# Seven of 64 scan inputs made by token: ScalarE scales dt * u by B, TensorE turns it back by channel

## What is computed

```python
xz = x @ W_in; x_in, z = split(xz)
u  = silu(conv4(x_in) + conv_b)                 # depthwise, 4 taps
Bm, Cm = split(u @ W_x)                         # 16 + 16 values a token
dt = softplus(u @ W_dt + b_dt)                  # 256 values a token
h  = exp(dt[:, :, None] * A) * h + (dt * u)[:, :, None] * B[:, None, :]   # for each token
y  = einsum('bdn,bn->bd', h, C)
y  = (y + u * D) * silu(z)
x  = layernorm(x + y @ W_out)
x  = layernorm(x + moe(x))                      # 8 experts, top 2, with a capacity
```

## Time and profile before

| | |
|---|---|
| runs | 399.35, 399.61, 401.03 us |
| profiled execution | 401.77 us, its span 400.0 us |
| busy, share of the span | TensorE 72%, VectorE 74%, ScalarE 48%, GpSimd 66% |
| granted TensorE clock, mean | 0.85 of full |
| start of unit 0's first scan | 24.7 us |
| end of the last scan | 269.3 us |
| experts on TensorE | 299 to 374 us |

### The profile page before, as it was taken

How to read it: one execution, slowest core, us unless ns; L and a number is a source line. 1 busy time by engine, 2 the same in 40 slices (tenths; PEclk the granted TensorE clock), 3 DMA queues, 4 the chain that set the end, 5 groups by cost and what they waited for, 6 DMA issues and landing times. The chain is left out here.

```text
span 400.0 us, 4740 instructions
## 1 busy us (share of the span) xinstructions
PE 286.7 (72%) x1420; PEld 200.4 (50%) x1420; DVE 296.2 (74%) x439; ACT 190.8 (48%) x372; POOL 265.0 (66%) x226
## 2 busy tenths in 40 slices
PE   8976888487785848595563897666089999999300
PEld 6435445364563434484351462223088888888300
DVE  2698899989999999889999999995212333333186
ACT  2846576575645694654544345571303333333105
POOL 4517488967788799988979885796520555555512
PEclk9998699979789868968555799899589999999955
DMA  7061069472344354122112311001152443224573
GB/s 209 22 211 52 2 234 277 120 220 86 84 146 122 104 145 156 66 67 95 63 61 69 122 66 54 0 13 42 34 149 68 124 125 116 86 77 131 145 216 105
DMA packets 35784, 42.87 MB, mean 107 GB/s; under 512 B 3862, under 2 KB 26331, under 8 KB 35760
## 3 DMA queue, kind: packets, MB, share of 16 engines
q1 hardware_dynamic: 32336, 37.38, 31.0%
q0 software_dynamic: 2304, 4.24, 3.2%
q10 hardware_dynamic: 1120, 0.97, 0.8%
HBM read 30.11 MB, written 12.79 MB: 107 GB/s over the span
## 5 line engine op out<-in xcount | busy, mean ns | idle before, releaser
L1265 POOL TENSOR_TENSOR product<-state,c_wide 128x1024 f32<-128x1024 f32 x64 | 149.8, 2345 | 50.2 <-DVE state L1493 30.2
L943 ACT ACTIVATE psum<-dt,a_neg 128x512 f32<-128x512 f32 x124 | 85.4, 690 | 99.9 <-DVE state L1493 96.9
L602 PE MATMUL psum<-ident,product 128*128 128x128 f32 x384 | 66.1, 330 | 36.9 <-POOL product L1265 36.8
L602 PEld LDWEIGHTS psum<-ident,product 128*128 128x128 f32 x384 | 55.4, 171 | 55.4 <-POOL product L1265 51.2
L1493 DVE TENSOR_TENSOR_SCAN state<-psum,carry,drive 128x512 f32<-128x512 f32 x64 | 79.9, 1275 | 2.0 <-ACT psum L943 1.8
L1472 DVE TENSOR_TENSOR drive<-dtu,psum 128x1024 f32<-128x1024 f32 x64 | 76.9, 1201 | 5.1 <-PE psum L588 4.9
L1493 DVE TENSOR_TENSOR_SCAN state<-psum,drive 128x512 f32<-128x512 f32 x64 | 75.7, 1212 | 3.2 <-ACT psum L943 2.7
L1386 POOL DMA_INDIRECT result_rows<-state,result_at x30 | 30.3, 1011 | 40.3 <-DVE state L1699 33.0
L1340 POOL DMA_INDIRECT slot_rows<-sent,scatter_at x32 | 32.6, 1020 | 10.9 <-issue 10.9
L804 PE MATMUL psum<-product,fc_sb 128*128 128x320 f32 x128 | 36.1, 435 | 1.1 <-DVE product L1675 1.1
L1672 DVE TENSOR_SCALAR tags<-c_wide 128x10 f32<-128x10 f32 x8 | 1.3, 164 | 43.0 <-PE psum L793 43.0
(11 more groups left out here) (239 smaller groups left out, 436.8 us busy)
## 6 DMA issues: line engine op xcount, KB each, us to landing
c_wide<-c_rows SPq DMA_DIRECT2D x32, 512.0 KB, 4.0
slot_rows<-blank SPq DMA_DIRECT2D x8, 325.0 KB, 4.8
c_wide<-slot_rows SPq DMA_DIRECT2D x8, 325.0 KB, 3.6
result_rows<-zeros SPq DMA_DIRECT2D x8, 256.0 KB, 5.2
late_rows<-zeros SPq DMA_DIRECT2D x8, 256.0 KB
fc_sb<-in_c_fc SPq DMA_DIRECT2D x8, 256.0 KB
proj_sb<-in_c_proj SPq DMA_DIRECT2D x8, 256.0 KB
c_wide<-result_rows SPq DMA_DIRECT2D x8, 256.0 KB
```

What stands on the lines that cost most here:

```text
L602: last = nc.tensor.matmul(y_part(j, d), product[:, i, d, j * P:(j + 1) * P], ident[:, :], is_transpose=True, start=False, stop=True, skip_ ...
L943: nc.scalar.activation(psum[:, A_BANK + d, :], dt[:, q % 2, d, :], ACT.Exp, scale=a_neg[:, n:n + 1]).then_inc(decay_ready, 1)
L1265: nc.gpsimd.tensor_tensor(product[:, U % PRODUCTS, channels, :], state[:, U % RING, channels, :], wide, ALU.mult).then_inc(product_ready, 1)
```

## The change

Seven units, 5, 8, 11, 14 in the first quarter and 52, 55, 58 in the last, get their drive by another way (`TURNED`). dt * u of the quarter is turned so that tokens lie on the partitions (`dtu_t`), and so are the rows of B (`b_t`); there B is one value per partition, and ScalarE multiplies (`drive_by_token`, four instructions of 128x256 a unit) into one buffer `drive_t`. TensorE turns the product back into the two banks of B, four transposes for each half (`turn_drive`), and the scan reads it from PSUM. The decay of such a unit is one 128x1024 instruction into SBUF (`decay_sb`). VectorE makes no drive for these units; the drive of the unit behind is made beside the scan of the unit in front (`drive_beside`). The spreads and drives are counted without the turned units (`drive_number`), and the spread of a unit behind a turned one also waits for the turned unit's scan, whose bank it takes. ScalarE issues the products of unit T at iteration T - 4, behind the wait for the transposes of the turned unit before T. `start_y(0)` moves from ahead of the loop into iteration 2, since its bank first holds the turned dt * u of quarter 0; that of quarter 3 is turned by two new jobs in iterations 44 and 46.

```diff
+TURNED = (5, 8, 11, 14, 52, 55, 58)
+def drive_number(U):
+    return U - sum(m < U for m in TURNED)
+def drive_beside(U):
+    if U in TURNED or U == LAST:
+        return None
+    return U + 2 if U + 1 in TURNED else U + 1
...
+        def b_bank(U):
+            return B_BANK + drive_number(U) % 2
+        def turned_bank(U, d):
+            return B_BANK + (drive_number(U) + 1 + d) % 2
...
+                ("t3a", 0), ("t3b", 0), ("y2a", 0), ("y2b", 1), ...
...
+            def turn_b(to):
+                for j in range(TPC):
+                    last = nc.tensor.transpose(to[:, j * D_STATE:(j + 1) * D_STATE], bc_sb[0:D_STATE, j * P:(j + 1) * P], ident[0:D_STATE, 0:D_STATE])
+                last.then_inc(b_turned, 1)
...
             part_dt(1, 1).then_inc(dt_projected, 1)
+            pe.wait_ge(bc_rows_ready, 1)
+            turn_b(b_t_psum(Z_BANK, 0))
             turn_x(3)
...
                 if U >= 2:
-                    pe.wait_ge(drive_ready, U - 1)
-                nc.tensor.matmul(psum[:, B_BANK + U % 2, :], selector[:, n, :], bc_parts[:, q * CH:(q + 1) * CH],
+                    pe.wait_ge(drive_ready, drive_number(U) - 1)
+                for d in range(DT):
+                    for T in range(U - 4, U):
+                        if T in TURNED and drive_number(U) == drive_number(T) + 1 + d:
+                            pe.wait_ge(scanned, DT * T + d + 1)
+                if U == 0:
+                    pe.wait_ge(b_t_ready, 1)
+                nc.tensor.matmul(psum[:, b_bank(U), :], selector[:, n, :], bc_parts[:, q * CH:(q + 1) * CH],
...
+            def turn_first_dtu():
+                pe.wait_ge(dtu_ready, DT)
+                for j in range(TPC):
+                    for d in range(DT):
+                        last = nc.tensor.transpose(y_part(j, d), dtu[:, 0, d, j * P:(j + 1) * P], ident[:, :])
+                last.then_inc(dtu_turned, 1)
+            def turn_drive(U, d):
+                pe.wait_ge(drive_t_ready, TPC * (TURNED.index(U) + 1))
+                pe.wait_ge(drive_ready, drive_number(U) + d)
+                for j in range(TPC):
+                    last = nc.tensor.transpose(psum[:, turned_bank(U, d), j * P:(j + 1) * P], drive_t[:, j, d * P:(d + 1) * P], ident[:, :])
+                last.then_inc(drive_turned, 1)
...
             spread_b(0)
             spread_b(1)
-            pe.wait_ge(diag_ready, DT)
-            start_y(0)
+            turn_first_dtu()
             pe.wait_ge(x_chan_ready[3], 1)
             for U in range(LAST + 1):
                 q, n = divmod(U, D_STATE)
-                if 2 <= U + 1 <= LAST:
-                    spread_b(U + 1)
+                if U == 2:
+                    pe.wait_ge(diag_ready, DT)
+                    pe.wait_ge(dtu_t_ready, 1)
+                    start_y(0)
+                if U in TURNED:
+                    turn_drive(U, 0)
+                    turn_drive(U, 1)
+                elif U >= 1 and U - 2 not in TURNED and drive_beside(U):
+                    spread_b(drive_beside(U))
...
                 for k in SUMS[q].get(n, []):
                     add_to_y(q * D_STATE + k)
+                if U - 1 in TURNED:
+                    spread_b(drive_beside(U + 1))
+                if q == 2 and n in (12, 14):
+                    dtu_job(3, (n - 12) // 2)
...
+                    if U in TURNED:
+                        if TURNED.index(U):
+                            act.wait_ge(scanned, DT * (TURNED[TURNED.index(U) - 1] + 1))
+                        nc.scalar.activation(decay_sb[:, :, :], dt[:, q % 2, :, :], ACT.Exp, scale=a_neg[:, n:n + 1]).then_inc(decay_ready, DT)
+                        break
                     if U:
-                        before = U - 2 if U - 1 in FAR else U - 1
+                        before = U - 2 if U - 1 in FAR + TURNED else U - 1
...
+            def drive_by_token(U):
+                q, n = divmod(U, D_STATE)
+                before = TURNED.index(U)
+                act.wait_ge(drive_turned, DT * before)
...
+                for j in range(TPC):
+                    nc.scalar.activation(drive_t[:, j, :], dtu_t[:, j, :], ACT.Copy, scale=b_t[:, j, n:n + 1]).then_inc(drive_t_ready, 1)
...
+                if U == 0:
+                    take_first_dtu()
                 if U < LAST and U + 1 not in FAR:
                     decays(U + 1)
                 keep_last(U)
+                if U + 4 in TURNED:
+                    drive_by_token(U + 4)
+                if q == 2 and n in (13, 15):
+                    take_dtu(3, (n - 13) // 2)
...
+                    decay = decay_sb[:, d, :] if U in TURNED else psum[:, A_BANK + d, :]
+                if U in TURNED:
+                    dve.wait_ge(drive_turned, DT * TURNED.index(U) + d + 1)
+                    rows = psum[:, turned_bank(U, d), :]
...
                 scan(U, 0)
-                if U < LAST:
-                    drives(U + 1)
+                if drive_beside(U):
+                    drives(drive_beside(U))
                 scan(U, 1)
```

68 lines of the change are left out of this document (59 added, 9 removed).

## The result

The changed kernel took 404.29 us in the median (402.60 to 405.31, six runs), the kernel before 399.79 beside it (399.19 to 401.48, six runs): ratio 1.0096, 95% interval 1.0073 to 1.0118, so slower by some 3.8 us; the medians lie 4.5 apart. The forecast was 401.6 us, +2.0. The direction came out; the price is about twice the one forecast.

The account below looks back on a forecast made before the run. VectorE's pace through 64 units, each one drive and two scans, was taken as the bound. First quarter +2.2, ahead of the scan +0.3, last quarter -0.5: +2.0 us on the median 399.61, so 401.6 us; range 396.0 to 405.3.

Parts of the forecast that it names:

- Added on ScalarE: Per turned unit: four multiplications of 0.39 us, 1.6 in all (ends 1.1 and 2.3), and one decay of about 1.05.
- Turned scans: VectorE's scans of turned units, operands swapped between PSUM and SBUF, keep 1.12 us each.
- Unit 5: First quarter: transposes behind TensorE's B/C projection; scan (5,0) at 46.6, not 44.1; (6,0) late by 1.8, (7,0) by 2.1.
- Unit 8: First quarter: transposes behind the late convolution matmul, VectorE loses 1.0 us; the decay of unit 9 makes (9,0) 3.7 late.
- Units 11 and 14: End of first quarter: 11 saves 1.0 us, 14 saves 0.5 because of GpSimd's queue; next quarter starts at 84.5, +2.2.
- Rival (b): GpSimd takes over from about 48.7: at most 2.3 us of VectorE's gains arrive; no change, 399.6 us; chance 0.2.
- Rival (c): TensorE stays at the lower clock between units 4 and 8: two more jobs add 3.4, 405.0 us, slower; chance 0.15.
- Ahead of the scan: Before the first drive: turning B's rows delays the first spread to 23.4 to 23.7; +0.3 us (0 to 0.6).
- Second and third quarter: Order stays; two turning jobs and their copies fall in ScalarE's waits for scans, adding nothing.
- Last quarter: Units 52, 55, 58: 2 us wait before scan 52, 55 saves 1.1, 58 loses its gain before the reciprocal; -0.5 us.
- -0.4 now: Last quarter: the running balance in us stated after unit 55 saves 1.1, the decay of 53 being 0.6 late.

Follow-up runs that it names:

- again: The changed kernel with nothing edited, run again for a second trace: 404.39 us to 400.08 for the kernel before, ratio 1.0103.
- after: The first profiled execution of the changed kernel, with all seven units turned: 402.60 us, the shortest of its six runs (median 404.29).
- prep_only: The changed kernel with no unit turned, all 64 drives on VectorE, the added preparation kept: 401.73 us to 400.08, ratio 1.0044.
- before_short: The kernel before with GpSimd's products of units 10 to 13 over 256 of 512 tokens: 399.02 us, ratio 1.0052.
- after_warm: The changed kernel with four idle 128x512 matmuls ahead of the B/C projection of iteration 4: 402.04 us to 400.27, ratio 1.0050.

## Why the prediction was right and wrong

**Added on ScalarE.** Right. Forecast 0.39 a piece and 1.6 us for four, with bounds of 1.1 and 2.3; measured 1.71 from the first to the end of the last, and 1.61 to the next start (47.53 to 49.14), 0.40 a piece. The estimate from the figures of the Trainium skill (ScalarE: Activation LUTs, What ACT_TABLE_LOAD costs) was 0.40 too, and this trace agrees. The decay took 1.14 where 1.05 was forecast.

**Turned scans.** Right: 2.33 a pair, 2.45 with the carry.

**Unit 5.** The mechanism is right and its size close, in the state of the earlier trace rows: (5,0) at 46.6 forecast, 47.15 in again; (6,0) at 50.3, 50.33; drive 7 at 51.95, 52.01. The half microsecond at (5,0): the scan starts 1.57 us after the first transpose, and I had 0.88 + 0.2.

**Unit 8.** Right: (8,0) at 58.5 forecast, 58.93 measured; (9,0) at 62.45, 62.78. So by unit 9 the loss was forecast as 3.7 us and was 4.0.

**Units 11 and 14, where the sum failed.** "11 saves 1.0", "14 saves 0.5", so unit 16 at 84.5. It came at 86.16. On VectorE the saving was there, as (15,0) started 2.6 us late and no longer 4.0. Then drive 16 waited 1.12. The gapless list of the earlier trace rows stood in the prediction, but it was taken as 3 us late at unit 14, with 11's saving already off, and not as 4: it has no gap from product 10 on, and dt * u, forecast for 75.7 by that, ran at 76.66. And the wait at drive 16, whose spread stands behind the sum of product 12, isn't in the prediction at all. The sum itself ran at the 1.2 GHz level (1.97 us for 1.09), 0.9 us of that wait. Rival (b) had the list as its mechanism and began it at 48.7: from there the list had gaps (1.00 before product 10, 1.85 before product 9 in again). What happened was the forecast's loss up to unit 9, and behind it the list together with TensorE's clock. What arrived of the two savings is 4.0 less 3.86, 0.1 to 0.2 us for 1.5, so this term is 1.3 us of the 1.8 to 2.5 that were missing.

**The clock.** Rival (c) was a lower clock between units 4 and 8, at +5.4. It wasn't so: the mean granted clock of the first quarter is 0.94 in after and 0.89 in again, against 0.88. What there was instead is a larger price of the same event, and one sum of a product at the lower level where it is on the path. The transposes follow the projection at whatever level it had (1.04 us for eight in after, 1.91 in again), and both are on the path now. The Trainium skill (TensorE: Matmul & The Clock Gate, Part 4: PE-mode transpose) has the upper level not engage for transposes; these rows show them at either level, so here the measurement decides. Whether transposes alone would bring the upper level, no run here shows.

**Ahead of the scan.** Wrong, by 0.3: no loss, unit 0's first scan started at 24.39 to 24.75 in the three traces, before at 24.72 and 24.63. The first spreads and the rows of B in after:

```profile
19.88 0.21 ACT L1020 ACTIVATE b_t<-psum 128x64 f32<-128x64 f32 x1
...
22.40 0.59 PE L641 MATMUL psum<-bc_parts,selector 128*128 128x512 bf16 x2
...
23.07 1.22 DVE L1613 TENSOR_TENSOR drive<-dtu,psum 128x1024 f32<-128x1024 f32 x1
```

I had the spread at 23.4 to 23.7, behind turning, x turn and convolution. The convolution started at 18.96, 1.5 later than in the earlier trace rows, but the spreads at 22.40, ahead of dt * u, which ends only at 23.03 and starts the drive. The step took for the limit what had slack.

**Second and third quarter.** Forecast zero. The sixteen traces with the preparation in them average 126.9 us between units 16 and 48 (125.5 to 127.9), the four of the kernel before, edited or not, 126.5 (126.1 to 126.8). That is 0.4 us, within the spread of single traces. The ratio of prep_only, 1.0044, says 1.7 us, and the trace doesn't locate them; after before_short, whose edit cost 0.5% without a wait to show for it, I take neither for a measured price of the preparation.

**Last quarter.** Right: (52,0) 17.2 us after the quarter's start forecast (226.05 less 208.88), 17.86 in after and 17.28 in again; waits of 2.73 and 2.14 for "2 us"; the reciprocal's 1.16 for "1 us". The eleven traces with 52, 55 and 58 turned average 58.7 us from unit 48 to the last scan, against 59.16: -0.5, as forecast (with 0.6 late and 1.1 saved the prediction's "-0.4 now" should read -0.5). That unit 55 saves 1.1 and unit 58 nothing came out too: in after it takes 7.01 us from unit 54 to 56 (8.16 in before) and 8.36 from 58 to 60 (8.39). TensorE and ScalarE in after, which answer to the earlier trace rows:

```profile
223.49 3.62 PE L618 MATMUL psum<-u,diag_d 128*128 128x512 f32 x4
226.90 1.34 PE L657 MATMUL psum<-ident,drive_t 128*128 128x128 f32 x8
...
228.28 1.70 ACT L1083 ACTIVATE drive_t<-dtu_t,b_t 128x256 f32<-128x256 f32 x4 [5.92 <-PE psum L657]
```

**The sum again**, with what was measured: first quarter +2.1 at the upper level of the clock and +3.8 at the lower, last quarter -0.5, +0.4 between, which no experiment supports by itself: +2.0 to +3.7. The three ratios give +3.8 to +4.4. The forecast was built on rows of the lower level, so +3.7 is what it should be held against, and of the 1.7 us between, 1.3 are units 11 and 14. That the number for the better level equals the forecast is chance. What the medians show beyond the parts, some tenths up to the half per cent by which they move in kernels whose traces show no reason, stays open, and so does the stretch behind the last scan, where traces of one chip lie up to 2.3 us apart.

## What to carry to other kernels

A saving on the engine that sets the pace arrives only as far as the next engine's list has gaps: follow that list from its last gap, not from the place of the edit, and then on through the engine that waits for it. Here 0.1 to 1.2 us of two savings came through, by the clock at which TensorE did the sums, and 1.9 with the list shortened. Before work goes to an idle engine, look at what its buffer waits for. With one buffer the idle engine becomes a link between two queues, and whatever stands behind it in its own queue is late as well; here a second buffer was worth 3.5 to 4.3 us in the times (1.5 to 3.0 located in the traces), and moving the transposes that started the wait 1.4. And where a stage runs at either clock level, work it out at both: a change that puts more of it on the path pays the difference every time the lower level comes.

## What the hardware showed

- One and the same job, four 128x512 float matmuls behind an idle time of 1.7 to 3.4 us, took 1.98 us in one execution and 3.78 in another of the same kernel (after and again); the one with the longer idle time was the slower here, but before_short took 1.98 behind 3.28. It decides 1.2 us of the unturned kernel and 2.8 of the turned one.
- Eight 128x128 matmuls that add a product to y took 1.09 us in one kernel and 1.97 in six others at the same place, behind a wait for GpSimd. With units 11 and 14 turned the way from (9,0) to unit 16 followed it: 22.37 us, and 23.39 to 23.41.
- Four idle matmuls in front brought the job to the upper level (1.88 us in after_warm) and gave back part of it: they take 3.60 us, 39.74 to 43.17 until the next start, where the job had started at 41.64 and 42.01.
- A wait of 1.5 to 2.0 us for a DMA ahead of a layer went with that layer at a lower clock (6.15 and 5.94 us for 4.54), and waits up to 0.72 us didn't.
- An edit that shortens four instructions of an engine with slack (before_short) raised the median by 0.5% (1.0024 to 1.0079); the cause is open.
